# Loads of input and context and the store of the attention's result, issued from GpSimd's queue in place of SyncE's, in a decoder layer on one Trainium2 core

## What is computed

```
x = x + attn(layernorm(x), Wq, bq, Wk, bk, Wv, bv, Wo, bo)
x = x + xattn(layernorm(x), ctx, ctx, mask, ...)      # scores = where(mask == 0, 1e-9, scores)
h = gelu(layernorm(x) @ ternary(W_fc).T)
x = x + layernorm(h, ln_w, ln_b) @ ternary(W_proj).T
```

## Time and profile before

| | |
|---|---|
| median of 3 runs | 2554.49 us (2551.3 to 2555.81) |
| profiled execution, its own time | 2553.16 us |
| its span in the trace | 2551.4 us |
| mean TensorE clock granted, share of full speed | 0.971 |
| PE busy | 2195.3 us (86%) |
| DVE busy | 2035.5 us (80%) |
| ACT busy | 1604.9 us (63%) |
| POOL busy | 1028.5 us (40%) |
| DMA moved | 277.01 MB, mean 109 GB/s |

### The profile page before, as it was taken

The page is one execution under the profiler, slowest core; times in us unless marked ns, Lnnn a source line. Parts: engine busy times, 40 slices in busy tenths (PEclk is TensorE's granted clock), DMA queues, the critical chain, the costliest instruction groups (busy, mean ns, idle before and its releaser), DMA issues.

```text
span 2551.4 us, 70786 instructions
## 1 busy us (share of the span) xinstructions
PE 2195.3 (86%) x29031; PEld 1445.0 (57%) x29031; DVE 2035.5 (80%) x4025; ACT 1604.9 (63%) x2354; POOL 1028.5 (40%) x719
## 2 busy tenths in 40 slices
PE   3668889888888888889888888889865899999999
PEld 1435555555555555555555555555533677777776
DVE  6558888888888888888888888888753688888887
ACT  2356666666666666666666666666532777878876
POOL 2133433443344344434433443343221455555553
PEclk7889999999999999999999999999987999999999
DMA  5266777667677666677766667677431233333332
GB/s 137 46 121 112 127 130 121 123 118 128 118 124 129 122 118 123 122 126 124 124 126 118 118 123 130 120 126 126 80 67 46 67 99 91 82 99 90 82 99 59
DMA packets 450784, 277.01 MB, mean 109 GB/s; under 512 B 299344, under 2 KB 401104, under 8 KB 450512
## 3 DMA queue, kind: packets, MB, share of 16 engines
q1 hardware_dynamic: 447408, 272.77, 56.8%
q10 hardware_dynamic: 3104, 0.34, 0.1%
HBM read 54.87 MB, written 33.55 MB: 35 GB/s over the span
## 4 chain that ended last, share of the span: by engine, by line
SPq 44%; PE 32%; DMA 10%; DVE 6%; issue 4%; ACT 3%; POOL 1%; DVEq 0%; ACTq 0%; POOLq 0%
SPq L593 37%; PE ybk L1355 9%; PE hbk L1379 8%; SPq L599 5%; DMA cross_stk<-cross_negmT 5%; PE tbk L1369 4%; PE product_bank L1024 4%; DMA self_stk<-self_negmT 4%; SPq L643 1%; PE score_bank L946 1%; PE score_bank L966 1%; PE exp_bank L946 1%; PE exp_bank L984 1%; DVE cross_mx L828 1%; PE product_bank L1031 1%
## 5 line engine op out<-in xcount | busy, mean ns | idle before, releaser
L730 ACT ACTIVATE prob<-exp_bank 128x1024 f32<-128x1024 f32 x512 | 523.0, 1021 | 288.2 <-PE exp_bank L984 283.8
L828 DVE TENSOR_REDUCE cross_mx<-score_bank 128x8 f32<-128x1024 f32 x256 | 311.2, 1216 | 138.4 <-PE score_bank L966 138.2
L662 POOL TENSOR_TENSOR xs<-xn,xs 128x1024 f16<-128x1024 f32 x64 | 136.2, 2128 | 686.7 <-ACT xs L757 686.7
L828 DVE TENSOR_REDUCE self_mx<-score_bank 128x8 f32<-128x1024 f32 x256 | 310.3, 1212 | 112.2 <-PE score_bank L966 112.2
L662 POOL TENSOR_TENSOR ahl<-attT,ahl 128x512 f16<-128x512 f32 x128 | 148.0, 1156 | 349.5 <-ACT ahl L735 349.4
L1379 PE MATMUL hbk<-wfcT,ffn_xhl 128*128 128x512 f16 x1024 | 262.2, 379 | 6.4 <-ACT hid L1276 3.6
L1339 DVE SCALAR_TENSOR_TENSOR ghl<-tbk,lnwc,ghl 128x512 f16<-128x512 f32 x256 | 188.0, 735 | 98.1 <-ACT ghl L1270 98.0
L1355 PE MATMUL ybk<-wpT,ghl 128*128 128x256 f16 x2048 | 260.5, 273 | 0.8 <-DVE ffn_y L1324 0.7
L1355 PEld LDWEIGHTS ybk<-wpT,ghl 128*128 128x128 f16 x2048 | 197.9, 98 | 66.0 <-DVE ghl L1339 0.9
L946 PE MATMUL exp_bank<-maskBT,pick 64*128 64x512 bf16 x1024 | 155.4, 382 | 74.6 <-ACT prob L730 35.4
L1270 ACT ACTIVATE ghl<-tbk,lnwc 128x512 f16<-128x512 f32 x256 | 174.0, 681 | 67.7 <-PE tbk L1369 67.7
(11 more groups left out here) (159 smaller groups left out, 4642.6 us busy)
## 6 DMA issues: line engine op xcount, KB each, us to landing
self_stk<-self_qk SPq DMA_DIRECT2D x768, 64.0 KB, 2.4
cross_stk<-cross_qk SPq DMA_DIRECT2D x768, 64.0 KB, 2.4
self_src<-in_x SPq DMA_DIRECT2D x32, 512.0 KB, 5.7
ctx_in<-in_ctx SPq DMA_DIRECT2D x32, 512.0 KB, 6.3
x_scratch<-xn SPq DMA_DIRECT2D x32, 512.0 KB, 5.5
ffn_src<-x_scratch SPq DMA_DIRECT2D x32, 512.0 KB, 3.8
out<-ffn_y SPq DMA_DIRECT2D x32, 512.0 KB, 3.6
self_stk<-self_negmT SPq DMA_DIRECT2D x64, 128.0 KB, 3.9
```

The source lines that it names most:

```text
L662: nc.gpsimd.tensor_tensor(out, src, hi, ALU.subtract).then_inc(lo_ready, 1)
L730: act.activation(prob[:, p % 3], ebank[:, :, :], ACT.Exp, scale=EXP_SCALE).then_inc(b.exp_done, 1)
L828: dve.tensor_reduce(a.mx[:, 8 * m:8 * m + 8].rearrange("p (j r) -> p r j", r=2), sbank[:, :, :].rearrange("p r (j k) -> p r j k", j=4), AX ...
```

## The change

The two loads and the store are issued from POOL. `load` and `store` move from `sp_slot` to `pool_slot`, where they stand behind `low_outputs(b, s.gb, 0)` and ahead of `deviations()`. The first loads (`load_first`) move from the head of SP's stream to the head of POOL's, ahead of the constants. Semaphores, tiles and sizes stay. PE, DVE and ACT have the same instructions in the same order as before.

```
         @block.sync
         def _(sp):
-            att.load_first(sp)
             prep.load_weights(sp)
...
         @block.gpsimd
         def _(pool):
+            att.load_first()
             prep.constants(pool)
...
             turn_input()
             stacks(2)
             maxima()
-            store()
-            load()
...
+            def load():
+                if b.cross:
+                    if s.gt is not None and present(s.gt + 1) is not None:
+                        x_group = x_groups[s.gt + 1]
+                        pool.wait_ge(slf.xb_ready, s.gt + 1)
+                        nc.gpsimd.dma_start(slf.src[:, :, :], x_group).then_inc(x_loaded, 16)
+                elif s.gt is not None and present(s.gt + 1) is not None:
+                    ctx_group = ctx_groups[s.gt + 1]
+                    pool.wait_ge(cs_lo, s.gt + 1)
+                    nc.gpsimd.dma_start(cin[:, :, :], ctx_group).then_inc(c_loaded, 16)
+
+            def store():
+                if a.cross and s.go is not None:
+                    x2_group = x2_groups[s.go]
+                    pool.wait_ge(crs.y_ready, s.go + 1)
+                    nc.gpsimd.dma_start(x2_group, xn[:, :, :]).then_inc(stored, 16)
...
             biased()
             low_outputs(b, s.gb, 0)
+            store()
+            load()
             deviations()
...
-        def load_first(sp):
-            sp.dma_start(slf.src[:, :, :], x_groups[0]).then_inc(x_loaded, 16)
-            sp.dma_start(cin[:, :, :], ctx_groups[0]).then_inc(c_loaded, 16)
+        def load_first():
+            nc.gpsimd.dma_start(slf.src[:, :, :], x_groups[0]).then_inc(x_loaded, 16)
+            nc.gpsimd.dma_start(cin[:, :, :], ctx_groups[0]).then_inc(c_loaded, 16)
```

More of the change, by code:

```diff
@@ L620, in stacks @@
                         stack_rows(sp, b, s.gq, 1 - s.rb, block)
[L622 to L637, removed]
             def maxima():
```

## The result

The changed kernel takes 2727.75 us (median of 4 runs, 2720.58 to 2744.62) against 2554.24 us for the kernel before (4 runs): a ratio of 1.0697, 95% interval 1.0661 to 1.0733. It is 7% slower. The direction was forecast; the size, 173 us where I had forecast 24, lies beyond the upper end of the range.

A forecast was written before the change was run, and what follows sets the result against it. SP's queue and the maxima's landing were taken to bound the attentions; issue terms counted 0, and 0.4 us a slot over 30 pairs added 24 us, giving 2578 us. Forecast's own range 2566 to 2602 us, overall range 2548 to 2628.

The forecast's parts named there:

- The loop: Attentions: SP's stacks, maxima landing, PE, ACT's output, next stacks; time on stack DMAs or landings returns one for one.
- SP's issues are worth 0: SP's queue: the three removed issues, 2.84 us a pair, lie in idle time and gain nothing.
- POOL's issue: POOL: three added issues a pair, taken as 1.2 us each, cost 0 up to 3.0 us each.
- The rival of long issues: POOL: describing a transfer takes over 3.0 us, delaying the self stacks; at 5 us, 2614 us; chance 0.08.
- The data beside the maxima: DMA queues: POOL's transfers flow beside the maxima and delay them 0.4 us a slot, 24 us in all.
- my own upper bounds: Maxima's delay if all other traffic goes ahead: 1.55 us in the even slot, 3.1 us in the odd.
- The two reasons for the smaller value: Maxima's delay: queues served in turn pass equal bytes, 0.77 us; part fits the gap left by slow maxima, so half.
- Completion held up by the other queue's writes: Maxima report completion only after POOL's earlier transfers are written: 2.4 us a pair, 72 us, 2626 us; chance 0.17.
- the sign that I had set: Profile after: maxima's chain pieces of 5 us and more speak for completion waiting on the other queue's writes.
- Nothing moves: DMA queues: POOL's traffic fits the gap left by slow maxima, time stays at 2554 us; chance 0.17.
- faster: Maxima land as if nothing followed, gaining 0.15 us (even) and 0.71 us (odd), 26 us, 2529 us; chance 0.14.

The follow-up runs named there:

- the run with both: Kernel before, with loads issued late from POOL in the next slot and the store on SP held until the cross maxima land: 2550.61 us, ratio 0.9950.
- the one with all issues on SP: Kernel before, but in odd slots SP waits for the maxima to land before issuing store and load: 2553.01 us, ratio 0.9949.
- the run with all on POOL: Changed kernel with loads moved to the next slot and the store right behind `residual`, ahead of `biased`: 2579.45 us, ratio 1.0058 to the kernel before.
- the store alone: Kernel before with only the store moved to POOL, both loads staying on SP: 2568.1 us, ratio 1.0043.
- The filler: Changed kernel plus 8 overwritten 128x512 products on PE ahead of its wait for the stacks: 2715.45 us, ratio 1.0583 to the kernel before.

## Why the prediction was wrong in size and right in direction

**The loop: right.** Maxima, exponentials, product, ACT, SP's next stacks pass on a delay. The chain shows the same loop in both kernels. For later landings it holds: they grew by 105 us in the chain, and nothing took that up but 44 us of SP's queue. For earlier ones it holds only in part: holding back the store took 0.69 us a pair off the cross maxima, 21 us, and the time fell by 11 to 13.

**SP's issues are worth 0: right.** With the loads off SP the time is 0.9995, and the run with both (0.9950) is no faster than the one with all issues on SP (0.9949). The context's transpose did get shorter, 2.87 us where it was 4.53, and SP then waited all the same.

**POOL's issue: right that it is hidden, and shorter than taken.** 0.75 to 0.81 us each where I had taken 1.2. The rival of long issues is out. That an issue is free holds for its place: ahead of `biased` it was not (the run with all on POOL).

**The data beside the maxima: the step that failed.** I wrote that "if the two queues are served in turn, the maxima's 256 KB let an equal amount past", 0.77 us, and took half of it, 0.4 us a slot. Measured over the chain's pieces, the self maxima went from 3.98 to 5.86 us (26 and 19 pieces) and the cross maxima from 4.47 to 6.90 (27 and 22): 1.9 and 2.4 us, against my 0.4. These are near my own upper bounds of 1.55 and 3.1 us, "all of the other traffic goes ahead"; the even slot is over its bound. The two reasons for the smaller value both fell. The maxima do not get an equal share of the bytes beside a load: 0.10 MB against 0.52 in the changed kernel, and 0.01 against 0.45 beside ACT's queue. And the gap that I saw in the maxima's 89 GB/s is no room: while the maxima move at a quarter of the rate, the DMA engines are 91% busy, and I had read that row and still counted the rate and not the share.
The Trainium skill says in "DMA: Bandwidth & Descriptors", section "Queues, rings and completion order", that a DMA engine takes its queues in turn, packet by packet, where a packet is a run of some 9 to 17 descriptors and at most 64. The trace neither confirms nor refutes it, for the profile counts smaller packets: with 96 transfers fewer, SP's queue has 50688 fewer, 528 for each transfer of 512 rows. A load has 512 rows over 16 DMA engines, 32 for each, so that, if a row is a descriptor, one to four turns carry a whole load. My error was to read "in turn" as equal bytes. What holds SP's packets back, the DMA engines' turns or what feeds them, no run here separates.

**What I had not looked for: the stacks ahead of the maxima.** POOL issues its load at 1049.86, when SP's last stack DMAs are still under way. The chain of the changed kernel has 15 pieces of stacks, some 78 us in all, 7 of the self stacks at a mean of 6.1 us and 8 of the cross stacks at 4.4; before it was 12 us in all, and the median landing of a stack is 2.4 us. I had placed the collision only at the maxima, and so had the stacks at nothing without a reason. They are 66 of the 105 us that landings add, the larger part, and landings are 105 of the 176.

**What I had not looked for: TensorE's clock.** A longer wait is followed by products at half clock that lie on the same chain; the sum had no term for them. Of the 84 us that PE gained in the chain, 52 are L1024's. The filler gave back some 29 us; how the 84 divide between clock and a chain that now runs through PE at places where SP's queue ran before (SP's share fell by 44 us) is not settled.

**The rivals.** Completion held up by the other queue's writes forecast 2.4 us a pair; the pair of slots lost 5.8 us (173 over 30). By the sign that I had set, pieces of 5 us and more, the run speaks for this rival; but the same sign comes from maxima whose data itself is late, and that is what the queues show for the loads: 0.10 MB until 1054, 0.45 MB behind it. For the store the rival wanted 1.1 us a pair, 33 us; the store alone cost 0.43%, 11 us, and its maxima landed in 4.50 us where it was 4.47. So the rival isn't needed; for the loads it is not excluded either. Nothing moves and faster are out. Faster had a true core, that the maxima gain 0.7 us where no store is behind them, but the way to it is to hold the store back on its own queue and not to give it another.

## What to carry to other kernels

Another issuing engine takes issuing time off a queue, but it also takes away the order between its transfers and those of the queue that they left. Where small transfers are on the path that sets the end, keep large ones behind them in the same queue, or hold them back until the small ones have landed; here that is the difference between 7% slower and 0.5% faster. Judge the room beside a transfer by the DMA engines' busy share and not by GB/s, and price a longer wait of TensorE with the slower clock that can follow it. Look at every transfer that is in flight when the new one starts, and not only at the one that the chain goes through now. And look at what stands behind the new issue on its engine: the issue makes that later, and with it whatever ends together with it.

## What the runs showed of the hardware that I had not expected

A large load from a second queue, GpSimd's or ScalarE's, passes almost alone: 0.52 MB against 0.10, and 0.45 MB against 0.01, while SP's queue has work. Beside a store from GpSimd's queue SP's queue moved 0.30 MB against 0.25. GpSimd needs about as long as SP to issue a 512 KB load (0.80 us, SP 0.73 and 1.43), and its packets are 3.6 KB where SP's and ACT's are 1 KB for the same transfer, which changed nothing in the cost (1.0697 and 1.0688). A wait of PE for a stack DMA, in which it was busy for 0.21 of 2.00 us, was followed by three microseconds at 1.2 GHz, and useless products in the wait made the kernel 1.1% faster. A DVE instruction of 128x64 elements took 1.09 us in one kernel and 2.13 us in another and in both ended 0.05 to 0.06 us behind a pass of POOL with which it shares no semaphore.
